# Moving the values' products ahead of the reciprocals' transposes on TensorE in a fused attention and expert kernel

## The reference

```python
x = x + jnp.tanh(g_xattn[0]) * xattn(layernorm(x), ctx, ctx)
#   qh, kh, vh: 16 heads of 16;  logits = qh kh^T / 4 + causal mask
#   attn = softmax(logits);  out = attn vh;  out @ dense_w.T + dense_b
x = x + jnp.tanh(g_ffn[0]) * ffn(layernorm(x))
#   router logits -> argmax expert, weight = its softmax probability
#   ffn = weight * (gelu(h w1[e] + b1[e]) w2[e] + b2[e])
```

## Time and profile before

| what | value |
|---|---|
| median of 3 runs | 541.25 us (540.46 to 541.8) |
| the profiled execution's own time | 542.62 us |
| its span, first to last instruction | 540.7 us |
| mean granted TensorE clock over the span | 0.962 |
| steps of blocks, first to last L947 | 28.8 to 325.0 us |
| PE, DVE, ACT, POOL busy, share of the span | 89%, 62%, 61%, 50% |

### The profile page before, as it was taken

The page is one execution under the profiler, slowest core; times in us unless marked ns, Lnnn a source line. Parts: engine busy times, 40 slices in busy tenths (PEclk is TensorE's granted clock), DMA queues, the critical chain, the costliest instruction groups (busy, mean ns, idle before and its releaser), DMA issues.

```text
span 540.7 us, 16942 instructions
## 1 busy us (share of the span) xinstructions
PE 482.0 (89%) x4893; PEld 418.6 (77%) x4894; DVE 336.3 (62%) x1046; ACT 330.9 (61%) x1459; POOL 271.0 (50%) x502
## 2 busy tenths in 40 slices
PE   2799999999999999999999986079999999999991
PEld 2578888878878878888788865069999999999880
DVE  1677788888888888888888885223434334343330
ACT  1589898988888888888788880022443334334230
POOL 5443436446545545555544634345556555665621
PEclk9999999999999999999999995569999999999997
DMA  7244645121121211212211011398988888988800
GB/s 246 57 169 136 205 141 147 53 69 43 49 68 45 56 54 49 60 46 51 66 39 39 21 41 40 49 308 288 274 264 292 273 272 264 284 279 242 284 10 1
DMA packets 37333, 72.65 MB, mean 134 GB/s; under 512 B 12585, under 2 KB 20911, under 8 KB 37296
## 3 DMA queue, kind: packets, MB, share of 16 engines
q10 hardware_dynamic: 7056, 29.72, 17.7%
q1 hardware_dynamic: 23184, 25.68, 16.5%
q0 software_dynamic: 7056, 16.79, 9.5%
HBM read 58.79 MB, written 15.07 MB: 137 GB/s over the span
## 4 chain that ended last, share of the span: by engine, by line
PE 66%; DVE 8%; issue 8%; ACT 6%; DMA 5%; POOL 3%; SPq 1%; DVEq 0%; POOLq 0%; ACTq 0%
PE bank L1042 14%; PE bank L1052 14%; PE bank L874 10%; PE bank L896 6%; PE bank L904 5%; ACT arena L533 5%; PE bank L972 5%; PE bank L980 4%; PE bank L947 2%; DMA arena<-token_rows,arena 2%; PE bank L888 2%; PE bank L1029 2%; DMA arena<-x 2%; POOL arena L435 1%; DVE stats L777 1%
## 5 line engine op out<-in xcount | busy, mean ns | idle before, releaser
L533 ACT ACTIVATE arena<-bank,negmax 128x128 f32<-128x128 f32 x512 | 180.4, 381 | 37.6 <-DVE negmax L647 36.3
L533 ACT ACTIVATION_READ_ACCUMULATOR arena<-bank,negmax 128x1 f32 x512 | 112.4, 219 | 0.0
L603 ACT ACTIVATE arena<-bank,w_ring 128x128 f32<-128x128 f32 x180 | 51.3, 368 | 85.1 <-PE bank L1042 72.3
L1042 PE MATMUL bank<-arena,w_ring 128*128 128x128 f32 x720 | 89.6, 279 | 0.6 <-DVE arena L827 0.6
L647 DVE TENSOR_REDUCE negmax<-bank 128x4 f32<-128x512 f32 x128 | 84.4, 681 | 8.7 <-PE bank L888 8.6
L1052 PE MATMUL bank<-W,arena 128*128 x360 | 85.9, 382 | 1.2 <-DVE arena L843 1.0
L1042 PEld LDWEIGHTS bank<-arena,w_ring 128*128 128x128 f32 x720 | 85.7, 195 | 1.0 <-issue 1.0
L843 DVE SCALAR_TENSOR_TENSOR arena<-bank,arena 128x256 f32<-128x256 f32 x45 | 21.8, 484 | 100.1 <-PE bank L1052 100.1
L896 PE MATMUL bank<-C,arena 128*128 128x128 f32 x512 | 73.8, 276 | 5.3 <-ACT arena L533 5.1
L874 PE MATMUL bank<-arena 128*128 128x128 f32 x512 | 72.4, 286 | 0.5 <-issue 0.5
L1052 PEld LDWEIGHTS bank<-W,arena 128*128 128x128 f32 x360 | 65.0, 191 | 8.9 <-issue 1.8
(11 more groups left out here) (109 smaller groups left out, 765.7 us busy)
## 6 DMA issues: line engine op xcount, KB each, us to landing
w_ring<-w1b ACTq DMA_DIRECT2D x45, 642.0 KB, 5.2
token_rows<-rows SPq DMA_DIRECT2D x32, 256.0 KB, 2.4
W<-w SPq DMA_DIRECT2D x14, 512.0 KB, 5.0
arena<-x SPq DMA_DIRECT2D x32, 128.0 KB, 2.1
arena<-ctxt SPq DMA_DIRECT2D x32, 128.0 KB, 2.2
arena<-token_names SPq DMA_DIRECT2D x45, 1.0 KB, 4.5
arena<-token_rows,arena POOLq DMA_INDIRECT x45, 4.4
out<-arena POOLq DMA_INDIRECT x45, 4.2
```

Source lines behind the costliest of these rows:

```text
L533: ins = act.activation(probs[:, q, v, :], bank[q][:, v * P:(v + 1) * P], ACT.Exp, bias=negmax[:, b.par, h:h + 1], accum_out=rsum[:, b.par, ...
L603: ins = act.activation(hid_t[:, k, ch, :], hid_bank[k][:, ch * P:(ch + 1) * P], ACT.Gelu, bias=w_ring[:, k, B1_AT + ch:B1_AT + ch + 1])
L1042: ins = pe.matmul(hid_bank[r][:, f * P:(f + 1) * P], w_ring[:, r, at:at + P], g_xt[:, r, ch, :], start=(ch == 0), stop=(ch == DC - 1))
```

## The change

On PE, `attend()` of block c with its two waits (`probs_t_vector`, `x2_ready`) is issued ahead of the two transposes of the reciprocals and their wait for POOL. The increment of `mixed_done` stays on the transposes, as the last instruction of the group. No instruction is added or taken away, and no other engine's program is touched. Lines from L955 on move up by one; the transposes of L947 are L951 in the new file, and L972, L980, L997 and L1003 are L971, L979, L996 and L1002.

```diff
@@ -942,16 +942,15 @@
                         ins = pe.matmul(at[:, r * E:(r + 1) * E], ones_bf[:, :], seen[:, :],
                                         start=False, stop=(r == 1))
                 if c.ok():
+
+                    pe.wait_ge(probs_t_vector, c.n * 2 + 2)
+                    wait(pe, x2_ready, c.n)
+                    attend()
                     pe.wait_ge(rinv_rep_ready, c.n + 1)
                     for ch in range(DC):
                         ins = pe.transpose(bank[5][:, ch * P:(ch + 1) * P], rinv_rep[:, ch * P:(ch + 1) * P], ident)
                 if c.ok() or e.ok() or (f.ok() and f.par == 1):
                     ins.then_inc(mixed_done, 1)
-                if c.ok():
-
-                    pe.wait_ge(probs_t_vector, c.n * 2 + 2)
-                    wait(pe, x2_ready, c.n)
-                    attend()
                 if a.ok():
```

## The result

The changed kernel takes 552.54 us (551.8 to 552.88, 4 runs) against 541.5 us, the median of the kernel before over four runs, one more than in the table above: the ratio is 1.0206, 95% interval 1.0188 to 1.0224. It is slower by 11.0 us, where 17.7 were forecast. The profiled execution took 552.75 us with a span of 550.8.

A forecast was written before the change was run, and what follows sets the result against it. Two loop cycles of almost equal length through PE's transposes, one via POOL, one via DVE's maxima and ACT's exponentials, were taken as bounds. Losses of 8.8 + 6.8 + 2.1 = 17.7 us gave 559.0 us, range 550 to 565.

The forecast's parts named there:

- the forecast's own: Whole kernel: the band around the forecast of 559.0 us, 553 to 564 us, given 72 in 100.
- only the written-out steps lose: Rival: the loop's DVE and ACT absorb their 0.44 us, 8.9 us of loss remain, 550.2 us; 12 in 100.
- ACT's wait ahead of quarter 1: Sign in the changed profile: ACT waits some 0.9 us ahead of the exponentials of quarter 1.
- the loop's step: Sign in the changed profile: a loop step grows from 9.8 us to about 10.25 us.
- The loop's term: Steps 12 to 31: even steps +0.32 us, odd +0.56, mean +0.44 over 20 steps, 8.8 us.
- The give-back at the first L655: Loop, DVE's copy of quarter 0 had waited for PE: 0.18 us back in even steps, 0.09 in odd.
- The last L896: Loop, PE's last transposes: follow the lateness of quarter 3's exponentials, 0.47 us in even steps, 0.56 in odd.
- The give-back at the scores' wait for POOL: Even loop steps: the scores' wait for POOL's masked keys should go, 0.15 us back.
- The written-out term: Steps 4 to 11: no wait for POOL to fill, 8 steps at 0.85 us, 6.8 us.
- The last blocks: Steps 32 to 34: between the loop's and the written-out steps' loss, estimated 3 x 0.7 = 2.1 us.
- TensorE's wait was what counted: Rival: only POOL's cycle is long, loop steps gain 0.35 us each, -7.0 us, 534.3 us; 4 in 100.
- the cancelling of gain and loss: Rival: a loop gain of some 9 us offsets the written-out steps' loss, no change; 2 in 100.

The follow-up runs named there:

- e1: Changed kernel, with DVE taking the maxima of quarter 1 ahead of its wait for mixed_done: 534.71 us, ratio 0.991.
- e5: Kernel before, with PE transposing quarter 1 ahead of the values instead of behind them: 535.87 us, ratio 0.9931.
- e2: Kernel before, with DVE taking the maxima of quarter 1 ahead of its wait for mixed_done: 540.76 us, ratio 1.0012.
- e4: Kernel before, with the change made in the 20 loop steps alone: 543.65 us, ratio 1.007.
- e9: Kernel before, with maxima of quarter 1 ahead of the wait in all steps, products ahead of the transposes in the loop alone: 535.15 us, ratio 0.9896.
- e6: Changed kernel, with quarter 1's maxima ahead of DVE's wait and quarter 1's transposes ahead of the values on PE: 536.07 us, ratio 0.9937.
- e11: Repeat of e1 (changed kernel, quarter 1's maxima ahead of DVE's wait) on the same chip as e9: 534.54 us, ratio 0.9882.
- e8: Kernel before, with quarter 1's maxima ahead of DVE's wait and quarter 1's transposes ahead of the values on PE: 536.05 us, ratio 0.9926.

## Why the prediction was right, and where its sizes were off

The direction and the mechanism held: DVE's path is the longer one, as the prediction had it. The increment of `mixed_done` came 0.68 us later in even and 0.59 in odd loop steps (0.65 forecast); ACT's quarter 1 came 0.67 and 0.58 later, with no slack, as read from the earlier trace rows; PE's queries came 0.43 and 0.52 us earlier and the win was lost in a wait at the last L896. e1 shows by taking it away that the place of a maximum behind the wait is the cause.

The sizes held less well. The measured 552.54 us lies in the range of 550 to 565, but just under the forecast's own 553 to 564, and nearer to the 550.2 of "only the written-out steps lose" than to the 559.0. ACT's wait ahead of quarter 1 was 0.71 us and not 0.9, PE's at the last L896 0.67 and not 1, and the loop's step 9.88 (even) and 10.05 us (odd) instead of 10.25. By the traces the loop and the first written-out steps were forecast 7.2 us too high, the last blocks 1.9 too low; that these offset each other in part is luck.

**The loop's term, 8.8 us, measured 3.5.** It is the largest miss: a step was forecast at 0.44 us and cost 0.17. Two parts of it were mis-sized.

- The give-back at the first L655. I took the bracket of 0.18 us in even steps and 0.09 in odd ones. Quarter 1 was late by 0.67 and 0.58, the first L655 by 0.41 in both, so 0.26 and 0.17 came back. I had counted from the recorded end of DVE's instruction before (0.18 us long), but in the changed kernel, where L655 needs not wait, it starts 0.08 to 0.09 us behind that one's start. The keys were late by 0.47 in even steps, as forecast, and by 0.41 in odd ones instead of 0.56.
- The last L896. I took its wait for one for ACT, so that it would be late by what ACT was. ACT's last exponential was late by 0.41 us in both kinds of step, L896 by 0.26 and 0.24 only, since before the change it had waited for DVE's second L655, and that came earlier. The view of waits names ACT for it (PEld L896, 3.7 us over 17 steps of the kernel before), whose last exponential ended close by; the PSUM bank in the code would have told. e5 shows the 0.15 us.

The give-back at the scores' wait for POOL in even steps (0.15 us) came as forecast: from L896 at 214.62 to L929 at 216.46 is 1.84 us instead of 2.01.

**The written-out term, 6.8 us, measured 5.0.** Steps 7 to 11 came as forecast, 0.82 us each. Steps 4 to 6 cost 0.28 instead of 0.85. The largest part of this is that the copy L673 stood behind maxima(0) on DVE, which the earlier trace rows don't hold:

```profile
47.02 0.69 DVE L647 TENSOR_REDUCE negmax<-bank 128x4 f32<-128x512 f32 x1 [1.33 <-PE bank L888]
47.63 0.41 DVE L673 COPY arena<-bank 128x256 f32<-128x256 f32 x1
```

There is no bracket ahead of L673: the transposes (46.88) were done 0.28 us before DVE was free. Only L929, from step 7 on, makes them late enough to be waited for. I had shifted L673 by the whole 1.01 us; in step 5 it came 0.73 later against the scores. The rest was given back in pieces on the way: the first L655 and maxima(3) were 0.54 us late, since L655 had waited for PE here too, which I had allowed for from step 7 on alone; quarter 3's first exponential 0.34, since it starts 0.72 us after maxima(3) and not the 0.80 that I had taken from a pair of maxima, and so had 0.20 us of slack; and the last L896 0.28.

**The last blocks, 2.1 us, measured 4.0.** Block 31's products were not in the sum at all. In step 35 nothing else is left to hide them. There the path goes from the products through the transposes, copy and L683, where before L683 followed the products directly. Besides, they ran at another clock. The products of before and of after:

```profile
325.29 1.41 PE L904 MATMUL bank<-arena 128*32 128x128 f32 x32
```
```profile
336.17 1.94 PE L904 MATMUL bank<-arena 128*32 128x128 f32 x32
```

And the stretches around them, in the view of busy time by stretch (the figure ahead of the DMA share is the granted clock, 1.00 being 2.4 GHz and 0.50 being 1.2 GHz):

```profile
324.00:326.00 2.00, 1.63 (x34) 1.46 (x38) 0.45 (x2) 0.60 (x2) 1.30 (x4) 0.97 0.04 8
```
```profile
336.00:338.00 2.00, 2.00 (x37) 1.54 (x37) 0.00 (x0) 0.00 (x0) 0.25 (x1) 0.50 0.03 8
```

Before, PE reached the products at 325.29, while the clock was still full, and it fell to half before they were through (0.72 over the products themselves); after, at 336.17, with the clock at half, and from there to the transposes took 1.87 us instead of 1.01. TensorE had waited for ACT several times in the last blocks in both kernels.

The other traces part the change from the clock. Where the last block's products ran at a granted clock of 1.00, from its L929 to the last L683 takes 2.12 us with the products behind the transposes (e2, e4, e5, e9) and 2.59 with them ahead (e1, e6, e11): the order costs 0.5 us. At half clock it takes 3.58 us with them behind (e8) and 3.98 ahead (the changed kernel); before it was 2.43. So of the 2.5 us in the table's last row 0.9 fall into step 34, 0.5 are the order, and 1.1 the clock, which was at half during these products in some kernels of either order. Why it fell in these and not in others stays open.

The rivals: that TensorE's wait was what counted is refuted for this order (the change itself is 11 us slower), and so is the cancelling of gain and loss. For this order the trace (552.5 us against 541.5) decides against the rule of the Trainium skill, page "Perfetto Trace Analysis", section "Optimization Strategies", that the matmul engine be kept as busy as possible. With one maximum taken ahead of the wait filling TensorE's wait does pay, with 0.35 us a loop step (e1 against e2), or 0.14 where quarter 1's transposes are early as well (e6 against e8). "Only the written-out steps lose" was nearest in size: 8.9 us were forecast for it, and the loop did lose much less than the sum had; but not nothing.

## What to carry to other kernels

Before work is put into a gap on one engine, follow the signal that stands behind the gap: what matters is who waits for it, and what of that engine's queue stands behind the wait without needing it. Here two maxima did, and moving one of them turned a loss of 11 us into a gain of 6. Where two instructions might release a third at nearly the same time, check the buffer as well as the data: the profile names one of them.

## What the runs showed of the hardware

In the loop of e1 ACT's exponentials start 0.34 to 0.36 us apart in a series, but the recorded length of one grows along an unbroken series: from 0.37 us at the first (198.19) to 0.42 at the twelfth, and 0.37 again after the keys:

```profile
201.97 0.42 ACT L533 ACTIVATE arena<-bank,negmax 128x128 f32<-128x128 f32 x1
...
202.50 0.63 ACT L563 ACTIVATE arena<-bank,arena 128x128 f32<-128x128 f32 x2
...
203.09 0.37 ACT L533 ACTIVATE arena<-bank,negmax 128x128 f32<-128x128 f32 x1
```

In e1 ACT had paused ahead of the keys, whose start is 0.53 us behind the last exponential's. In the changed kernel they follow at 0.34 us (212.16 to 212.50) without a pause, and the exponential behind them is recorded with 0.39 us (213.04), hardly less than the 0.40 of the twelfth. So here a pause brought the length back, and the keys alone did not.

The lag from the last exponential to the L896 that waits for it is not explained by this: it was 0.54 us in the even loop step shown of the changed kernel and 0.62 in its written-out step 5 (45.00 to 45.62), with 0.39 us recorded for the exponential in both. Why stays open.
